# Ten second-layer groups send their attention output through DRAM, with SP sending the sums first and both w_out halves of batches 0 and 1 in one key tile

## The reference

```python
xn = layer_norm(x, norm_w, norm_b)
q, k = xn @ q_w + q_b, xn @ k_w + k_b          # 16 heads
att = einsum('bnhl,bmhl->bnmh', q, k) + (1 - mask) * -1e6
att = softmax(att, axis=2)
v = (xn @ v_w + v_b) * mask
y = einsum('bnmh,bmhl->bnhl', att, v)
scale, shift = split(silu(emb) @ emb_w + emb_b, 2)
h = layer_norm(y, sb_norm_w, sb_norm_b) * (1 + scale) + shift
out = x + silu(h) @ out_w + out_b
```

## Time and profile before

| | us |
|---|---|
| median of 3 runs | 491.29 (490.81 to 492.58) |
| the profiled execution | 491.88 |
| its span, first to last instruction | 489.7 |
| PE busy | 478.3 |
| DVE busy | 385.4 |
| ACT busy | 342.3 |
| POOL busy | 313.6 |

### The profile page before, as it was taken

The page is one execution under the profiler, slowest core; times in us unless marked ns, Lnnn a source line. Parts: engine busy times, 40 slices in busy tenths (PEclk is TensorE's granted clock), DMA queues, the critical chain, the costliest instruction groups (busy, mean ns, idle before and its releaser), DMA issues.

```text
span 489.7 us, 9703 instructions
## 1 busy us (share of the span) xinstructions
PE 478.3 (98%) x3197; PEld 179.7 (37%) x3197; DVE 385.4 (79%) x989; ACT 342.3 (70%) x677; POOL 313.6 (64%) x445
## 2 busy tenths in 40 slices
PE   7999899999999999999999999999999999999996
PEld 3553322322443325332443235334333323333234
DVE  3767896999886796859776698867899999999124
ACT  2662567898667785968667785776787788777853
POOL 5569976899885996789646792859990055005501
PEclk9999999999999999999999999999999999999999
DMA  7775156355322465225502361114311121111011
GB/s 255 200 199 190 48 170 228 112 154 157 117 66 68 126 172 152 62 80 139 151 13 69 110 182 46 46 39 116 108 46 44 45 88 45 44 46 45 1 44 44
DMA packets 41577, 49.79 MB, mean 102 GB/s; under 512 B 12388, under 2 KB 34036, under 8 KB 41272
## 3 DMA queue, kind: packets, MB, share of 16 engines
q1 hardware_dynamic: 33336, 31.84, 22.2%
q0 software_dynamic: 7904, 16.03, 11.3%
q10 hardware_dynamic: 288, 1.31, 0.8%
HBM read 27.62 MB, written 19.01 MB: 95 GB/s over the span
## 4 chain that ended last, share of the span: by engine, by line
PE 74%; DVE 12%; POOL 5%; issue 3%; DMA 2%; ACT 1%; SPq 0%; DVEq 0%; POOLq 0%; ACTq 0%
PE bank L596 18%; PE bank L642 11%; PE bank L570 10%; PE bank L579 10%; PE bank L558 9%; DVE masked L955 7%; PE bank L653 6%; PE bank L670 5%; DVE row_max L958 2%; PE bank L627 2%; POOL XN L930 1%; DMA sums<-oT 1%; PE bank L611 1%; ACT probs L780 1%; PE bank L604 1%
## 5 line engine op out<-in xcount | busy, mean ns | idle before, releaser
L780 ACT ACTIVATE probs<-bank 128x512 f32<-128x512 f32 x512 | 269.3, 600 | 71.7 <-PE bank L570 70.9
L958 DVE TENSOR_REDUCE row_max<-bank 128x1 f32<-128x512 f32 x256 | 159.4, 681 | 34.0 <-PE bank L579 33.7
L579 PE MATMUL bank<-k_s,q_s 64*128 64x512 f16 x512 | 178.7, 382 | 2.3 <-DVE row_max L958 1.2
L955 DVE CUSTOM_DVE_ANT_0 masked<-bank,mask_bias 128x512 bf16<-128x512 f32 x256 | 161.7, 686 | 19.2 <-PE bank L579 18.7
L558 PE MATMUL bank<-q_s,k_s 64*128 64x512 f16 x512 | 151.4, 380 | 0.3
L570 PE MATMUL bank<-shift,kx 64*128 64x512 f16 x512 | 148.7, 376 | 0.4 <-DMA shift<-shift_rows 0.4
L596 PE MATMUL bank<-probs,v_aug 128*17 128x512 f32 x1024 | 135.5, 598 | 0.7 <-ACT probs L780 0.7
L579 PEld LDWEIGHTS bank<-k_s,q_s 64*128 64x128 f16 x512 | 46.2, 93 | 157.1 <-DVE row_max L958 70.9
L642 PE MATMUL bank<-xT,wqkv 128*128 128x512 f32 x128 | 59.6, 606 | 1.0 <-DVE xT L1096 0.6
L570 PEld LDWEIGHTS bank<-shift,kx 64*128 64x128 f16 x512 | 46.8, 95 | 34.1 <-DMA shift<-shift_rows 0.9
L1236 POOL TENSOR_SCALAR scaled<-row_max 128x16 f32<-128x16 f32 x30 | 7.7, 255 | 79.9 <-DVE row_max L955 44.5
(11 more groups left out here) (123 smaller groups left out, 478.9 us busy)
## 6 DMA issues: line engine op xcount, KB each, us to landing
q_s<-q_parts SPq DMA_DIRECT2D x32, 256.0 KB, 3.2
k_s<-k_parts SPq DMA_DIRECT2D x32, 256.0 KB, 4.1
k_parts<-parts POOLq DMA_DIRECT2D x62, 128.0 KB, 3.1
q_parts<-parts POOLq DMA_DIRECT2D x60, 128.0 KB, 3.0
X<-in_x SPq DMA_DIRECT2D x4, 512.0 KB, 7.3
O<-oT SPq DMA_DIRECT2D x64, 32.0 KB, 2.0
roped<-inverses SPq DMA_DIRECT2D x16, 128.0 KB
y<-X SPq DMA_DIRECT2D x7, 256.0 KB, 2.2
```

Of the source, the lines that this page charges most:

```text
L579: nc.tensor.matmul(bank, m.q_s[slot][rows, i, queries], m.k_s[slot][rows, i, :], start=True, stop=True).then_inc(q.d_made, 1)
L780: act.activation(m.probs[k][:, h, :], bank, ACT.Exp, scale=1.0 if s >= B * NG else float(DH) ** -0.5)\
L955: dve.tensor_tensor_reduce(m.masked[D["max", n, k, h] % ND][:, :], bank, m.mask_bias[:, b, :], 1.0, LOWEST, ALU.add, ALU.max, to)\
L958: dve.tensor_reduce(to, bank, AX.X, ALU.max).then_inc(q.d_done, 1)
```

## The change

A constant SENT = 26 marks the groups whose output goes the way of layer 0: groups 16 to 25 join 0 to 15. For these ten, PE's four transposes of `oT`, DVE's reciprocal and its product are gone. SP sends sums, channels and inverses as in layer 0; POOL inverts the sums by pow with exponent -1 on 128x16 and multiplies in place (`divide`). Since tokens are wanted, PE turns each finished half of the channels back by four transposes (pieces "back", five in all) and ACT copies them, 128x512, into `m.tokens`, two halves of the weight tile `wc`, which takes the place of `O` for layer 1.

SP sends sums ahead of the operand loads; inverses_in moves from the end of an iteration to the head of the next in layer 0 and stands at the end in layer 1; the tile of sums is doubled. The pieces of steps 20 to 28 move: both y halves of batches 0 and 1 stand in the tile in which the statistics of batches 1 and 2 are taken, tiles (25, 3) and (28, 3). POOL's order in layer 1 is written out anew.

```diff
+SENT = LAYER + NG * (B - 2) + NG // 2
-PIECES[20] = ((), qk(1, LAST, 2, 3), (), v(1, LAST))
-PIECES[22] = (*one(turn("f1", 0)), (), ())
-PIECES[23] = ((), (), y(1, 0)[:1], ())
-PIECES[24] = ((), (), (), y(1, 0)[1:])
-PIECES[26] = (*one(turn("f1", 1)), (), ())
-PIECES[27] = ((), (), y(1, 1)[:1], ())
-PIECES[28] = ((), (), (), y(1, 1)[1:])
+PIECES[20] = ((), qk(1, LAST, 2, 3) + (("back", 0, 0),), (), ())
+PIECES[21] = ((), (), (("back", 0, 1),), v(1, LAST))
+PIECES[23] = (*one(turn("f1", 0)), (), (("back", 1, 0),))
+PIECES[25] = ((), (), (("back", 1, 1),), y(1, 0))
+PIECES[27] = (*one(turn("f1", 1)), (), ())
+PIECES[28] = ((), (), (("back", 2, 0),), y(1, 1))
...
-for _b in range(B - 1):
-    STATISTICS[20 + NG * _b, 3] = ("f1", _b)
+for _b, _s in enumerate((21, 25, 28)):
+    STATISTICS[_s, 3] = ("f1", _b)
...
-        if op == "output" and k == 2 and s > LAYER:
+        if op == "output" and k == 2 and s > SENT:
...
+    def turn_back(piece):
+        _, b, c = piece
+        bank = a_free(A[piece])
+        pe.wait_ge(q.divided, normalised(B + b, c))
+        for t in range(TPB):
+            last = nc.tensor.transpose(bank[:, t * P:(t + 1) * P], m.raw[b % 2][:, c, t * P:(t + 1) * P], m.ident[:, :])
+        last.then_inc(q.a_made, 1)
...
+    def back(piece):
+        _, b, c = piece
+        bank = made(A[piece])
+        if b >= 2:
+            act.wait_ge(q.xn_made, TPB * NORMAL.index(("f1", b - 2)))
+        act.activation(m.tokens[b % 2][:, :, c * P:(c + 1) * P], bank.rearrange("p (t n) -> p t n", n=P), ACT.Copy)\
+            .then_inc(q.a_done, 1)
...
+    def divide(pu, c):
+
+        layer, b = divmod(pu, B)
+        pool.wait_ge(q.output_out, group_out(NG * pu + 2 * c + 1))
+        pool.wait_ge(q.inv_in[c], 32 * (pu + 1))
+        to = raw = m.raw[b % 2][:, c, :]
...
+        pool.tensor_tensor(to, raw, m.inverse[c][:, :], ALU.mult).then_inc(q.divided, 1)
+
+    def invert(s):
+
+        pool.wait_ge(q.sums_in, 16 * (s + 1))
+        pool.wait_ge(q.inv_out, 16 * s)
+        pool.tensor_tensor(m.inv_sum[:, :, :, :].rearrange("p t h w -> p (t h w)"), m.sums[s % 2][:, :], m.minus_one[:, :],
+                           ALU.pow).then_inc(q.inv_made, 1)
...
+    invert(16)
+    invert(17)
+    normalise(LAST)
+    divide(B, 0)
+    add_output_bias(LAST)
+    add_bias(LAST - 1, 0)
+    invert(18)
+    add_bias(LAST - 1, 1)
+    negate(21)
+    split(B + LAST, 0)
+    split(B + LAST, 1)
+    invert(19)
+    negate(22)
+    divide(B, 1)
+    invert(20)
+    split(B + LAST, 2)
+    split(B + LAST, 3)
+    negate(23)
+    rstd("f1", 0)
+    normal("f1", 0)
+    invert(21)
+    negate(24)
+    divide(B + 1, 0)
+    silu(0)
+    negate(25)
+    invert(22)
+    invert(23)
+    add_bias(LAST, 0)
+    negate(26)
+    divide(B + 1, 1)
+    invert(24)
+    add_bias(LAST, 1)
+    negate(27)
+    rstd("f1", 1)
+    normal("f1", 1)
+    invert(25)
+    negate(28)
+    divide(B + 2, 0)
+    silu(1)
+    negate(29)
...
     def sums(s):
 
         sp.wait_ge(q.acc_copied, s + 1)
-        if s:
-            sp.wait_ge(q.inv_made, s)
+        if s >= 2:
+            sp.wait_ge(q.inv_made, s - 1)
...
+        if 1 < s <= LAYER + 1:
+
+            inverses_in(s - 2)
+        if 0 < s <= SENT:
+            sums(s - 1)
         if 0 < s and exists(s + 3):
             operands(s + 3)
-        if 0 < s <= LAYER:
-            sums(s - 1)
         if exists(s + 1):
             shift(s + 1)
-        if 0 < s <= LAYER:
+        if 0 < s <= SENT:
             raw_output(s - 1)
...
-        if 0 < s <= LAYER:
+        if 0 < s <= SENT:
             inverses_out(s - 1)
+        if LAYER < s <= SENT:
             inverses_in(s - 1)
```

More of the change, by code:

```diff
@@ L191, in key_tile @@
                 yield "piece", piece
-        if op == "output" and k == 2 and s > LAYER:
+        if op == "output" and k == 2 and s > SENT:
             yield op, s - 1
-        if op == "output" and k == 3 and 0 < s <= LAYER:
+        if op == "output" and k == 3 and 0 < s <= SENT:
             yield "sums", s - 1
@@ L278, in chunk_rows, with normalised @@
     return slice(G * DH * (g % 2), G * DH * (g % 2 + 1))
-def normalised(b, c):
-    return CT * b + c + 1
+def normalised(pu, c):
+    return CT * pu + c + 1
 def await_shift(engine, q, n):
@@ L369, in build @@
         m.wc = sb("wc", [P, KC, COND])
+        m.tokens = [m.wc[:, 2 * i:2 * i + 2, :].rearrange("p k n -> p (k n)").rearrange("p (t c) -> p t c", c=C)
+                    for i in range(2)]
         m.vb_row = sb("vb_row", [P, C])
@@ L401, in build @@
         m.inverse = [m.roped[0][1], m.roped[1][1]]
-        m.sums = sb("sums", [P, KT * G])
+        m.sums = [sb(f"sums{i}", [P, KT * G]) for i in range(2)]
         m.parts = sb("parts", [P, 2, 4, 512], F16)
@@ L430, in build @@
         q.inv_made = sem("inv_made")
+        q.one_made = sem("one_made")
         q.xn_made = sem("xn_made")
@@ L752, in tensor @@
                 turn_tokens(piece)
+            if piece[0] == "back":
+                turn_back(piece)
             if piece[0] == "qk":
@@ L909, in scalar @@
                 tokens(piece)
+            if piece[0] == "back":
+                back(piece)
             if piece[0] == "qk":
@@ L974, in invert @@
             dve.wait_ge(q.inv_out, 16 * s)
-        dve.reciprocal(m.inv_sum[:, :, :, :].rearrange("p t h w -> p (t h w)"), m.sums[:, :]).then_inc(q.inv_made, 1)
+        dve.reciprocal(m.inv_sum[:, :, :, :].rearrange("p t h w -> p (t h w)"), m.sums[s % 2][:, :]).then_inc(q.inv_made, 1)
     def write_output(s):
@@ L979, in write_output @@
         bank = made(D["output", s]).rearrange("p (t h w) -> p t h w", t=KT, h=G)
[L980 to L984, removed]
+        if s == SENT:
+            dve.wait_ge(q.inv_out, 16 * SENT)
+        if s == SENT or g == 0:
             dve.wait_ge(q.xn_made, TPB * NORMAL.index(("f1", pu - 2 - B)))
-        if s > LAYER:
+        if s > SENT:
             dve.wait_ge(q.d_done, D["output", s - 1] + 1)
@@ L1018, in take_statistics @@
         else:
-            dve.wait_ge(q.d_done, D["output", NG * (B + b) + NG - 1] + 1)
-            statistics(kind, b, lambda t: m.O[b % 2][:, t, :])
+            dve.wait_ge(q.a_done, max(A[piece] for piece in A if piece[:2] == ("back", b)) + 1)
+            if NG * (B + b) + NG > SENT:
+                dve.wait_ge(q.d_done, D["output", NG * (B + b) + NG - 1] + 1)
+            statistics(kind, b, lambda t: m.tokens[b % 2][:, t, :])
         aggregate(kind, b)
@@ L1113, in last_batch @@
     def last_batch():
-        O = m.O[LAST % 2]
+        O = m.tokens[LAST % 2]
         steps = [TPB]
@@ L1173, in vector @@
                 negate(n)
-        if op == "sums":
+        if op == "sums" and at[0] < LAYER:
             invert(*at)
@@ L1180, in vector @@
                 for t in range(TPB):
-                    dve.bn_stats(m.last_stats[:, t, 0, :], m.O[LAST % 2][:, t, 0:EARLY]).then_inc(q.last_step, 1)
+                    dve.bn_stats(m.last_stats[:, t, 0, :], m.tokens[LAST % 2][:, t, 0:EARLY]).then_inc(q.last_step, 1)
         if op == "statistics":
@@ L1211, in normal @@
             await_turned(pool, q, NORMAL[n - 2])
-        src = m.O[b % 2] if kind == "f1" else m.X[:, TPB * b:TPB * b + TPB, :]
+        src = m.tokens[b % 2] if kind == "f1" else m.X[:, TPB * b:TPB * b + TPB, :]
         for t in range(TPB):
@@ L1310, in add_bias @@
                                m.v_tmp[:, t, :].rearrange("p (h d) -> p h d", d=DH), ALU.add).then_inc(q.v_made, 1)
[L1312 to L1319, removed]
+    def divide(pu, c):
[3 more added lines that the diff above has]
+        to = raw = m.raw[b % 2][:, c, :]
+        if layer == 0:
+            use = USES.index(("f0", b))
+            await_read(pool, q, use - 2)
+            to = m.xT[use % 2][:, c, :]
+        pool.tensor_tensor(to, raw, m.inverse[c][:, :], ALU.mult).then_inc(q.divided, 1)
[4 more added lines that the diff above has]
+                           ALU.pow).then_inc(q.inv_made, 1)
     moments_order = []
@@ L1457, in gpsimd, with silu @@
             modulation()
[L1458 to L1474, removed]
+    def silu(b):
         for h in range(CT):
@@ L1479, in gpsimd @@
             pool.tensor_tensor(m.xT[i][:, h, :], m.tanh[h], m.halved[h], ALU.mult).then_inc(q.silu_made, 1)
-        for n in (NG * (B + b) + 8, NG * (B + b) + 9):
-            if n in POOL_SHIFTS:
-                negate(n)
+    pool.wait_ge(q.one_made, 1)
+    invert(16)
[38 more added lines that the diff above has]
+    negate(29)
+    negate(GROUPS - 2)
+    rstd("f1", 2)
+    normal("f1", 2)
+    negate(GROUPS - 1)
+    silu(2)
     for p in range(PAIRS):
@@ L1557, in raw_output @@
         sp.wait_ge(q.acc_copied, s + 1)
-        if b >= 2:
+        if b >= B + 2:
+            sp.wait_ge(q.a_made, A["back", b - 2 - B, g // 2] + 1)
+        elif b >= 2:
             sp.wait_ge(q.divided, normalised(b - 2, g // 2))
```

12 lines of the change are left out of this document (7 added, 5 removed).

## The result

| | before | after |
|---|---|---|
| median, us | 491.94 (490.81 to 494.16, 4 runs) | 497.25 (495.86 to 498.09, 4 runs) |
| ratio | | 1.0117 (95% interval 1.0097 to 1.0137) |
| profiled execution / its span, us | 491.88 / 489.7 | 495.86 / 494.0 |

I had forecast 492.2 with a range up to 497.0. The time lies just above the range, on the side of rival 2.

The account below looks back on a forecast made before the run. PE and DVE were taken to bound the kernel about equally; 4.2 us of gains against 5.1 of stalls from replaying POOL's order gave 0.9 longer, stated as 492.2 us (forecast chance 0.42), range 486.6 to 497.0.

Parts of the forecast that it names:

- rival 2: SP stands at inverses_out waiting for POOL, so transfers behind it reach step 25 late: 494.3 or 495.5 us, chance 0.26.
- the gain of lighter tiles: PE in layer 1: ten outputs removed (6.2 us), five back pieces added (3.1), y halves put together (0.6 gained).
- The straight step of pow: POOL's pow on 128x16, extended at 0.165 us an element from widths 2 and 4: 3.0 us, bounds 1.0 and 4.2.
- rival 1: POOL's inversion is cheap, so no stall and the whole 4.2 us gain stays: 487.1 us, chance 0.28.
- A: PE at the back piece of step 21, tile (21, 2), waits for POOL's divide: 0.6 us.
- B: PE at the start of step 25, tile (25, 0), waits for shift rows: 3.0 us.
- C: PE at the end of tile (25, 1) waits for POOL's shift 26: 1.0 us.
- D: PE in tile (25, 2) waits for POOL's divide: 0.5 us.
- Rival 3: DVE stays the bound, so the removed transposes are not paid back and half of 6.2 is lost: 495.3 us, chance 0.04.
- landing of the sums: Transfer on SP's queue that POOL's layer 1 inversion waits for: taken as 2.0 us.
- landing of the inverse brought in: Transfer on SP's queue that POOL's divide waits for: taken as 3.4 us, bounds 2.6 and 4.5.
- The 0.5 for SP's order: First layer, sums ahead of operand loads removes DVE's wait in step 13: 0.5 us less, bounds 0 and 1.3.

Follow-up runs that it names:

- run 6: The kernel before with both y halves of batches 0 and 1 in one tile each, (24, 3) and (28, 3): 490.09 us, before 490.78, ratio 0.9980.
- run 3: The changed kernel with POOL's inversion 22, then shift 25, moved ahead of the silu of batch 0: 492.53 us, before 490.96, ratio 1.0033.
- run 7: The changed kernel with SP sending the shift rows ahead of the operand loads: 503.73 us, before 490.78, ratio 1.0253.
- run 8: The changed kernel with its ten inversions on DVE, and SP sending shift rows ahead of operand loads: 497.80 us, before 490.78, ratio 1.0132.
- run 5: The kernel before with only SP's order changed, sums ahead of the operand loads: 490.68 us, before 490.78, ratio 1.0.
- run 1: The changed kernel with POOL multiplying the sums by -1 instead of pow, leaving the ten inversions out: 488.88 us, before 490.96, ratio 0.9974.
- run 4: The changed kernel with twelve products of zeros added on PE at the start of step 25: 498.15 us, before 490.96, ratio 1.0156.
- run 9: The changed kernel with pow on 8 of 16 columns of each inversion, a product by -1 on the rest: 492.80 us, before 491.46, ratio 1.0036.

## Why the prediction was wrong, by its steps

**Right.** What bounds the kernel: the tiles without an output went to 2.51, the gain of lighter tiles was 3.9 for 3.7, and the y products gave 0.7 for 0.6 (run 6). That the gain fits so well is in part luck, two errors that cancel: an output or a back piece that shares its tile with other pieces costs 0.43 to 0.44 there and not 0.62 (outputs in tiles (18, 2) and (19, 2), back pieces in (20, 1) and (28, 2)), so the outputs gave some 5.8 for 6.2 and the back pieces took 2.7 for 3.1. The straight step of pow: 2.93 for 3.0. The Trainium skill's 2.6 cycles an element (GPSIMD Engine Reference, section 3.1), by which I had an estimate of 0.22, does not hold for pow; the trace disagrees by a factor of 13, and rival 1 fell with it. The mechanism: stalls A, B and C are at the named tiles with the named releasers, B behind inverses_out(22) (in run 3 it is gone); D hardly came (0.05). Rival 3 fell as well.

**The step that failed is the landing of the sums.** I took 2.0 us, "between the 1.5 of the inverse out and the 2.8 of the loads", two other transfers. Measured from the issue to the inversion that waited for it: 3.44 (301.60 to 305.04) and 3.55 (387.37 to 390.92) in after. The trace of before had a row of this very transfer. The sums for which DVE waited until 237.75 had been issued here:

```profile
231.92 0.61 SPq L1552 DMA_DIRECT2D sums<-oT  x1
```

That is 5.8 us, behind two operand loads: another place in the queue, and so no measure of what came, but no ground for 2.0 either, and I had priced this stall without asking how long its landing was. The second size is the **landing of the inverse brought in**, 3.4 taken, 3.7 to 4.9 measured in the four waits of after, 3.7 to 4.0 in those that bear on a stall. Two of these pairs, SP's issue and POOL's start:

```profile
342.52 0.61 SPq L1646 DMA_DIRECT2D roped<-inverses  x1
...
370.60 0.62 SPq L1646 DMA_DIRECT2D roped<-inverses  x1
```

```profile
346.50 1.27 POOL L1350 TENSOR_TENSOR O<-O,roped 128x512 f32<-128x512 f32 x1 [4.16 <-DMA roped<-inverses]
...
374.33 1.28 POOL L1350 TENSOR_TENSOR O<-O,roped 128x512 f32<-128x512 f32 x1 [4.25 <-DMA roped<-inverses]
```

Before had said 4.5 at 261.26, and three more of its divides stood idle behind an inverse just issued: 4.8 (149.31), 4.2 (204.21) and 4.1 (234.11). Those rows put the idle time down to "issue" and name no transfer, so each is a reading and not a measured landing, but all four lie above my 3.4, which leaned on loads in a quiet part. My replay, done again with 2.93 for the inversion, 3.45 for the sums and 3.8 for the inverse, has stalls of 1.85 at (21, 2), 3.68, 2.19 and 0.42 in step 25: 8.2, against 5.1 with my sizes and 7.9 measured at these four tiles. The sums weigh most: worked through by the steps of the prediction, 2.93 with 3.45 alone gives about 7.5, and 2.93 with 3.8 alone about 5.8. That these two sizes are the miss rests on this replay, an estimate from the measured rows; no run changes a landing by itself.

**The sum again.** Between the profiled executions I had 0.9 more and found 4.3. Of the 3.4 between them 2.8 are the four stalls (7.9 for 5.1), 1.0 are stalls that I had at nothing, 0.2 the start of the span; step 13 gave 0.4 and the lighter tiles 0.2 more than predicted. The 1.0 is shift rows late in step 18 (0.80) and a small stall in tile (24, 1): "Operands issued some 2 us later are needed only a step later: nothing" overlooked that shift rows queue behind the loads; runs 7 and 8 show how little room there is either way. The 0.5 for SP's order came from one profiled execution and is 0.1 between medians (run 5), so I took a stall of some executions for one of all. The medians lie 5.3 apart, 1.0 more than the spans of the profiled executions; after's profiled execution is the shortest of its four, 1.4 below their median, and no trace shows what the longer ones do. The long executions of runs 1 and 4 had late shift rows in step 18 and a fallen clock behind them, which may be the same; it was not seen in the changed kernel.

**The range.** Rival 2 had the right mechanism, and my replay varied the inversion and the inverse's landing for it, but kept the sums at 2.0 in every case. Both landings stand in one loop (sums, inversion, inverse out and in, SP free, next sums), so their errors add up and show in each pass. With 4.5 and 2.8, both rows that I had named, the replay has 9.8 of stalls, which is 5.6 more than before and 496.9; with 3.5 for the sums 11.2 and 498.3. By these rows the upper end belonged above 498, and rival 2 above its 0.26.

## What to carry to other kernels

Read a landing from the rows of that same transfer, from its issue to the first instruction that waits for it, also where the wait was short or hidden; a transfer of similar size elsewhere is no bound. Where work is moved into a loop between engines through a queue that works in order, list what stands behind each wait of the queue and vary every term of the loop at once; a queue can stand behind an engine that is a third idle. The remedy here was the place of the slow operation (0.25 us on DVE, 2.93 on POOL), not the order of the transfers.

## What was not expected of the hardware

- pow on POOL, 128 partitions: 0.71 us at 2 elements, 1.04 at 4, 1.66 at 8 (run 9), 2.93 at 16: a straight line of about 0.16 an element.
- A transfer of 8 KB on SP's queue (the sums) took 3.1 to 3.9 us to release its waiter (eleven waits in after and runs 1, 3, 4, 7 and 9), hardly less where the loads beside it left later (run 7: 3.1 and 3.5), while inverses of the same size went out in a median of 1.5. The page of the Trainium skill on transfers, DMA: Bandwidth & Descriptors (Anatomy of one DMA), has a fixed 2.0 us plus the bytes for GpSimd's transfers; by it 8 KB would be about 2.0, an estimate, and on SP's queue, which that figure is not for, the sums are far above and the inverses below.
- The granted clock fell to 1.2 GHz after standstills of PE of 3.38 (after), 2.39 (run 1), 2.19 (run 9) and 2.67, 2.40 and 2.00 us (run 4), and not after 1.80 (after, step 21). It cost 1.5 us in a tile that PE sets (run 1; 1.6 at the same place in run 4) and nothing that could be seen where POOL ended the tile.
